# The expert stage of a four-layer network as one unrolled stream, with the gathers in fp32r

## The reference

```python
x = x + _L0_ffn_ref(_L0_cond_ref(x, cond, ...), gate_w, w1, w2)   # layer 0
x = x + _L1_ffn_ref(_L1_cond_ref(x, cond, ...), ...)             # layers 1 to 3
...
def _L0_ffn_ref(x, gate_w, w1, w2):
    probs = softmax(einsum('BTC,CE->BTE', x, gate_w))
    top_p, top_idx = top_k(transpose(probs, (0, 2, 1)), cap)   # cap = 2*32/8 = 8 tokens for each expert
    xin = take_along_axis(x[:, None], top_idx[..., None], axis=2)
    h = gelu(einsum('BElC,ECH->BElH', xin, w1))                # 8 experts, H = 512
    y = einsum('BElH,EHC->BElC', h, w2) * top_p[..., None]
    return zeros.at[b_idx, top_idx].add(y)
```

## Time and profile before

| | |
|---|---|
| time, 3 runs | median 617.47 us (617.43 to 617.65) |
| the profiled execution | 614.02 us |
| its span, first to last instruction | 612.7 us |
| mean granted TensorE clock | 0.989 of full |
| TensorE busy | 568.9 us (93%) |
| VectorE busy | 444.6 us (73%) |
| ScalarE busy | 359.5 us (59%) |
| GpSimd busy | 206.6 us (34%) |

### The profile page before, as it was taken

One profiled execution on the slowest core, in us unless ns is written; L12 is line 12 of the kernel. 1 busy time (PEld: TensorE's weight loads), 2 busy tenths in 40 slices (PEclk: granted clock), 3 DMA queues, 4 the chain that ended last, 5 costly groups with the idle time before them and its releaser, 6 DMA issues.

```text
span 612.7 us, 10503 instructions
## 1 busy us (share of the span) xinstructions
PE 568.9 (93%) x3463; PEld 486.2 (79%) x3479; DVE 444.6 (73%) x1080; ACT 359.5 (59%) x773; POOL 206.6 (34%) x200
## 2 busy tenths in 40 slices
PE   8988999999998698999899978999999999999995
PEld 7766788787876587998789967789889898988773
DVE  5966555555565767675765625998999999999965
ACT  5456666775775332443233324587677777778873
POOL 5757777877865002976100000011000000001110
PEclk9999999999998799999899999999999999999999
DMA  8613304441300341013000000000000000000001
GB/s 293 207 71 142 139 17 192 172 172 67 140 1 19 119 147 51 1 53 104 0 0 0 1 1 1 2 1 2 2 1 10 19 10 10 11 10 10 19 18 34
DMA packets 13929, 34.72 MB, mean 57 GB/s; under 512 B 3148, under 2 KB 6584, under 8 KB 12984
## 3 DMA queue, kind: packets, MB, share of 16 engines
q1 hardware_dynamic: 13880, 34.10, 15.5%
HBM read 30.24 MB, written 2.28 MB: 53 GB/s over the span
## 4 chain that ended last, share of the span: by engine, by line
PE 74%; DVE 8%; POOL 6%; ACT 5%; issue 4%; DMA 2%; SPq 1%; DVEq 0%; ACTq 0%
PE bank L366 8%; PE bank L368 7%; PE bank L367 7%; PE bank L1259 7%; PE bank L1476 4%; PE bank L1468 4%; PE bank L1555 4%; PE bank L1500 4%; PE bank L1501 3%; POOL hidden_low L418 3%; PE bank L1347 3%; PE bank L1167 2%; POOL hidden_low L982 2%; PE bank L1534 1%; PE bank L1521 1%
## 5 line engine op out<-in xcount | busy, mean ns | idle before, releaser
L418 POOL TENSOR_TENSOR hidden_low<-hidden,hidden_high 128x512 fp32r<-128x512 f32 x72 | 92.3, 1294 | 31.2 <-ACT hidden_high L413 30.4
L1832 POOL CAST h_high<-h 128x256 fp32r<-128x256 f32 x16 | 7.3, 459 | 207.5 <-ACT h L1644 207.5
L483 ACT ACTIVATE bank<-bank 128x512 f32<-128x512 f32 x56 | 32.6, 583 | 36.6 <-PE bank L368 36.4
L487 DVE TENSOR_TENSOR hidden<-bank,big 128x512 f32<-128x512 f32 x56 | 38.5, 688 | 21.4 <-ACT bank L483 20.7
L366 PE MATMUL bank<-xin_high,w_high 128*128 128x256 f32 x128 | 46.5, 363 | 6.5 <-DVE xin_low L1236 6.5
L413 ACT CAST hidden_high<-hidden 128x512 fp32r<-128x512 f32 x73 | 44.9, 615 | 3.8 <-DVE hidden L479 3.0
L1500 PE MATMUL bank<-taps_high,q1T 128*128 128x512 f32 x94 | 45.6, 486 | 0.8 <-DVE tap L1740 0.5
L1287 ACT ACTIVATE pb<-bank 128x512 f32<-128x512 f32 x32 | 19.1, 597 | 35.1 <-PE bank L368 34.9
L1501 PE MATMUL bank<-taps_low,q1T 128*128 128x512 f32 x94 | 37.0, 394 | 0.0
L1468 PE MATMUL bank<-x,lstm_wx 128*128 128x128 f32 x256 | 33.7, 275 | 2.9 <-ACT ident_bf L1449 1.9
L368 PE MATMUL bank<-xin_high,w_low 128*128 128x256 f32 x128 | 36.3, 284 | 0.0
(11 more groups left out here) (274 smaller groups left out, 1788.0 us busy)
## 6 DMA issues: line engine op xcount, KB each, us to landing
big<-gates_scratch SPq DMA_DIRECT2D x7, 2048.0 KB, 7.5
w<-in_f_w SPq DMA_DIRECT2D x16, 256.0 KB, 7.7
onehot<-topi_scratch SPq DMA_DIRECT2D x6, 512.0 KB, 3.8
outT<-x SPq DMA_DIRECT2D x16, 128.0 KB, 1.8
xT<-in_xT SPq DMA_DIRECT2D x3, 512.0 KB, 8.0
cgt<-ctok SPq DMA_DIRECT2D x6, 256.0 KB, 4.6
big<-topi_scratch SPq DMA_DIRECT2D x2, 512.0 KB, 4.4
hidden<-in_ffn_w SPq DMA_DIRECT2D x3, 256.0 KB, 2.9
```

Of the source, the lines that this page charges most:

```text
L418: pool.tensor_tensor(hidden_hl[u % 3][1][:, :], hidden[u % 3][:, :], hidden_hl[u % 3][0][:, :].bitcast(F32), ALU.subtract).then_inc(s_lo, 1)
L487: dve.tensor_tensor(hidden[u % 3][:, :].rearrange("p (i k) -> p i k", k=P), r_bank[j % 2][:, :].rearrange("p (i k) -> p i k", k=P), gate_r ...
```

## The change

It does the following.

1. Lin, `val`, the loop and the DMA copies `cgt` go; all four groups are written out as one stream of 64 units, w = 16 g + u. `expert_up` runs LEAD = 3 units ahead, across the borders of groups.
2. The tail of group g: half of the transposes (experts 0 to 3) behind unit 14, the other half behind unit 0 of group g+1, the scatter behind its unit 2. Each half is one round through both banks.
3. The choice of half 0 moves from chunk 7 to chunk 5; its loads are issued in chunk 6. The first gather moves into chunk 7, behind units 7, 9 and 10, the fourth part behind the last unit. The choice of half 1 moves into group 0.
4. A gather multiplies the high and the low part of the tokens with the one-hot rows in fp32r, into two banks; a ScalarE copy of each bank gives the high and the low part of the gathered tokens. So `expert_split` splits only weights, and the tokens are split once per half group: high part on ScalarE (in chunk 7 on VectorE), low part on VectorE. `GATHER_AFTER` is 5, 7, 9, 11.

The core of the diff (renamings, and `val(...)` around constants, left out):

```diff
@@ chunk @@
+            CHOICE_CHUNK, LAST_GATHER = 5, (7, 9, 10)
+                    if last and u in LAST_GATHER:
+                        if u == LAST_GATHER[0]:
+                            pe.wait_ge(s_q, NCHUNK * NSH - 1)
+                        gather_product(LAST_GATHER.index(u))
-                    if last and u == 3:
+                    if c == CHOICE_CHUNK and u == 3:
                         choice_exp(0)
+                    if last and u >= 10:
+                        gather_copy(u - 10)
                 if last:
                     hidden_high(c, n - 1, units[n - 1])
+                    gather_copy(2)
...
+                    if last and u in (1, 2):
+                        gather_onehot(0, u - 1)
+                    if last and u in (4, 5):
+                        tokens_high(dve, 0, u - 4)
+                        tokens_low(0, u - 4)
+                    if last and u >= 10:
+                        expert_split(u - 10)
-                    if last and u >= 9:
+                    if c == CHOICE_CHUNK and u >= 9:
                         choice_tables(0, ...)
...
+                if c == CHOICE_CHUNK:
+                    choice_store(0)
+                if c == CHOICE_CHUNK + 1:
+                    sp.wait_ge(s_vc, 32)
+                    for k in range(2):
+                        gather_loads(0, k)
+                    load_slots(0)
@@ gather, units @@
+            LEAD = 3
+            def gather_product(q):
+                g, par, b = q // 4, (q // 2) % 2, q % 2
+                pe.wait_ge(s_oh, q // 2 + 1)
+                pe.wait_ge(s_cs, 2 * (q // 2) + 2)
+                if q:
+                    pe.wait_ge(s_gx, q)
+                for i in range(2):
+                    tile = 2 * b + i
+                    slots = slice(tile * SLOT_TILE, (tile + 1) * SLOT_TILE)
+                    for half, dst in zip(tokens(g, par), gather_banks(q)):
+                        mm = pe.matmul(dst[:, i * SLOT_TILE:(i + 1) * SLOT_TILE], half[:, tile * C:(tile + 1) * C],
+                                       chosen(g, par)[:, slots], start=True, stop=True)
+                mm.then_inc(s_ga2, 1)
+            def gather_copy(q):
+                act.wait_ge(s_ga2, q + 1)
+                for k in range(2):
+                    ...
+                    cp = act.copy(..., gather_banks(q)[k][:, :].rearrange("p (i e s) -> p e i s", i=2, e=E))
+                cp.then_inc(s_gx, 1)
+            def expert_split(k):
+                e = k % E
+                if k >= 2:
+                    dve.wait_ge(s_h, 2 * k - 2)
+                high, low = w1_hl[e % 2]
+                dve.tensor_copy(high[:, :], w1[:, e, :]).then_inc(s_es, 1)
+                dve.wait_ge(s_es, 2 * k + 1)
+                dve.tensor_tensor(low[:, :], w1[:, e, :], high[:, :].bitcast(F32), ALU.subtract).then_inc(s_es, 1)
@@ stream @@
+            def group_pe(g):
+                for u in range(U2):
+                    w = g * U2 + u
+                    if w + LEAD < GROUPS * U2:
+                        expert_up(w + LEAD)
+                    if g == 0 and u == 2:
+                        pe.wait_ge(s_sce, NCHUNK)
+                    if g == 0 and u == 4:
+                        pe.wait_ge(s_ye, 1)
+                        choice_transpose(1, y_bank[0][:, SLOT_GE:SLOT_GE + P])
+                    if g == 0 and u == 8:
+                        pe.wait_ge(s_dc, TABLES + TURNED)
+                    expert_down(w)
+                    if g and u == 0:
+                        slots_turn(g - 1, 1)
+                    if g and u == 2:
+                        scatter(g - 1, 0)
+                        scatter(g - 1, 1)
+                    if g < GROUPS - 1 and u in GATHER_AFTER:
+                        ...
+                        gather_product(q)
+                    if g == 0 and u == 12:
+                        pe.wait_ge(s_gx, 8)
+                        weight_total(m_bank[1][:, 0:4])
+                    ...
+                    if u == 14:
+                        slots_turn(g, 0)
+            def group_act(g):
+                for u in range(U2):
+                    w = g * U2 + u
+                    ...
+                    act.activation(hb[w % 4][:, :], h_bank[w % 4][:, :], ACT.Gelu).then_inc(s_hg, 1)
+                    if g == 0 and u == 1:
+                        choice_exp(1)
+                    if g < GROUPS - 1 and u in (2, 6):
+                        tokens_high(act, g + 1, u // 4)
+                    if g and u == 3:
+                        slots_out(g - 1, 1)
+                    if g < GROUPS - 1 and u - LEAD in GATHER_AFTER:
+                        gather_copy(4 * (g + 1) + GATHER_AFTER[u - LEAD])
+                slots_out(g, 0)
+            def group_dve(g):
+                for e in range(E):
+                    k = g * E + e
+                    if k + 2 < GROUPS * E:
+                        expert_split(k + 2)
+                    if g and e == 1:
+                        residual(g - 1, 0)
+                        residual(g - 1, 1)
+                    if g < GROUPS - 1:
+                        if e in (1, 3):
+                            tokens_low(g + 1, e // 2)
+                        if e in (2, 4):
+                            gather_onehot(g + 1, e // 2 - 1)
+                    if e >= 4:
+                        scatter_tables(g, range(4 * (e - 4), 4 * (e - 3)))
+                    output_copy(g, e)
+                    if g == 0 and e == 0:
+                        choice_probs(1)
+                        slots_copy(0, m_bank[0])
+                    if g == 0 and e == 2:
+                        choice_tables(1, y_bank[0][:, SLOT_GE:SLOT_GE + P], (0, 1))
+                    if g == 0 and e == 3:
+                        choice_tables(1, None, (2, 3))
+                    if g == 0 and e == 5:
+                        weight_sums()
+                    if g == 0 and e == 6:
+                        weight_means(m_bank[1][:, 0:4])
-            with nc.Fori(0, GROUPS - 2) as i:
-                group(Lin(i, 1, 1))
```

More of the change, by code:

```diff
@@ new lines, in gather_onehot, with half_tokens, tokens_high @@
+            def gather_onehot(g, par):
+                dve.wait_ge(s_ld[par], 16 * (g + 1))
+                dst = chosen(g, par)
+                dve.tensor_scalar(dst, dst.bitcast(F32), part[:, 0:1], None, ALU.is_equal).then_inc(s_oh, 1)
+            def half_tokens(g, par):
+                k = 2 * g + par
+                return ctok[:, k * HALF_TILES:(k + 1) * HALF_TILES, :].rearrange("p i c -> p (i c)")
+            def tokens_high(eng, g, par):
+                k = 2 * g + par
+                if g >= 2:
+                    eng.wait_ge(s_ga2, 2 * k - 2)
+                eng.wait_ge(s_cs, 2 * k)
+                cast = eng.copy if eng is act else eng.tensor_copy
+                cast(tokens(g, par)[0], half_tokens(g, par)).then_inc(s_cs, 1)
@@ new lines, in expert_down @@
+            def expert_down(w):
+                e, b = (w % U2) // 2, w % 2
+                pe.wait_ge(s_hg, w + 1)
+                if b == 0 and w >= 4:
+                    pe.wait_ge(s_ye, w // 2 - 1)
+                for i in range(2):
+                    ht = 2 * b + i
+                    mm = pe.matmul(y_bank[e % 2][:, 0:SLOT_GE], w2[:, e, ht, :], hb[w % 4][:, i * SLOT_GE:(i + 1) * SLOT_GE],
+                                   start=(ht == 0), stop=(ht == HT - 1))
+                mm.then_inc(s_y2, 1)
@@ new lines, in slots_out, with scatter @@
+            def slots_out(g, h):
+                for b in range(2):
+                    act.wait_ge(s_yt, 4 * g + 2 * h + b + 1)
+                    if g and h == 0 and b == 0:
+                        act.wait_ge(s_so, 2 * g)
+                    dst = ysl[:, 8 * b:8 * b + 8, :].rearrange("p (i h) k -> p i h k", h=2)[:, :, h, :]
+                    act.copy(dst, m_bank[b][:, :].rearrange("p (i k) -> p i k", k=P)).then_inc(s_yl, 1)
+            def scatter(g, b):
+                pe.wait_ge(s_yl, 4 * g + 4)
+                pe.wait_ge(s_st, 2 * g + b + 1)
+                for i in range(4):
+                    tile = 4 * b + i
+                    for h in range(2):
+                        mm = pe.matmul(m_bank[b][:, i * P:(i + 1) * P], ysl[:, 2 * tile + h, :], scat[:, 2 * tile + h, :],
+                                       start=(h == 0), stop=(h == 1))
+                mm.then_inc(s_so, 1)
@@ new lines, in build_program @@
+            for w in range(LEAD):
+                expert_up(w)
+            for g in range(GROUPS):
+                group_sp(g)
+                group_pe(g)
+                group_act(g)
+                group_dve(g)
+                if g == 0:
+                    prepare_weights()
+                if g == GROUPS - 2:
+                    for k in range(3):
+                        load_tap(k)
+            slots_turn(GROUPS - 1, 1)
+            slots_out(GROUPS - 1, 1)
+            for b in range(2):
+                scatter(GROUPS - 1, b)
```

(1 more changed line is left out.)

468 lines of the change are left out of this document (189 added, 279 removed).

## The result

The changed kernel takes 598.89 us (median of 4 runs, 597.71 to 599.28), the kernel before 617.45 in the same comparison: ratio 0.9697, 95% interval 0.9681 to 0.9714. The forecast was 600.3. The profiled execution took 598.74 with a span of 597.4 (before 614.02 and 612.7).

A forecast was written before the change was run, and what follows sets the result against it. TensorE, busy 93% of the span, was taken as the bound. Savings 10.8 - 1.1 - 1.0 - 1.3 + 9.8 = 17.2 us gave 596.8 profiled; carrying 3.45 to the median gave 600.3, range 594 to 608.

The forecast's parts named there:

- Between the stages: Gap from the last chunk product to the first expert product: 14.2 us falls to 3.4, 10.8 saved.
- low clock: First expert products may still run at half rate for 1 to 5 us: 1.0 us lost, bounds 0 and 2.5.
- The exponential ... moved, so nothing: Half 0's exponential, moved from chunk 7 to 5: two table loads and TensorE's 1.33 us wait only move, net cost nothing.
- token splits: Two splits at 1.15 us, with two one-hot tables at 0.66, in chunk 7: 1.3 us lost together, bounds 0 and 2.8.
- Top-k: Half 0's top-k tables stand between units in chunk 5: 1.0 us lost, bounds 0 and 2.4.
- gather copies: Two ScalarE copies of 1.08 us each ahead of the last chunk's last two hidden casts: 1.1 us lost.
- Lead of 3 and group 0: Late weight splits cost TensorE 1.7 us in groups 1 to 3; group 0 waits 5.2, ending at 36.2.
- fp32r gathers: Each gather block in the expert groups costs TensorE 0.48 us, not 0.87: 4.7 us saved over 12 blocks.
- A: Rival: VectorE bounds the expert stream, its split 0.35 us late for all 32 experts: 607.8 us; chance 0.18.
- B: Rival: moved VectorE work hides in idle time and group 0's waits are half the predicted: 595.4 us; chance 0.20.
- C: Rival: group 0's waits make the clock fall and stay low for the group: 631 us; chance 0.04.
- D: Rival: SP's queue brings one-hot rows 8 us late in chunk 7 and again in group 0: 616.3 us; chance 0.04.

The follow-up runs named there:

- tokens_early: Changed kernel with the token splits for the first gather placed one by one in chunk 4, not in chunk 7: 596.95 us.
- x_later: Changed kernel with, in chunk 5 alone, the split of x for the next chunk behind unit 6, not unit 3: 597.25 us.
- early split: Changed kernel with VectorE splitting the weights of expert k+3, not k+2, ahead of the output copy of expert k: 592.85 us.
- lead of 2: Changed kernel with LEAD = 2 in place of 3, nothing else: 592.20 us.
- tails_end: Changed kernel with transposes, scatter and addition to x of groups 0 to 2 at the end of their own group: 608.78 us.
- best 1: Changed kernel plus early split, x_later, first three gather copies behind the last hidden cast, and half 0's top-k spread over four units: 589.75 us.
- best 2: best 1 plus tokens_early and the weight total of group 0 behind unit 13, not 12: 586.47 us.

## Why the prediction was right, and where it was not

- **Between the stages:** right, and more: 12.2 saved, not 10.8. The transposes and scores ran at clock 1.00, not 0.50; probably because the first gathers fill idle pieces ahead of the end, which no run shows by itself. The "low clock" term (1.0) did not come here either. Low clock came in chunks 5 and 6 instead (0.8), where the prediction had none.
- **"The exponential ... moved, so nothing"** is the step that failed. It cost 3.37 in chunk 5 (the run without its tables takes all of it out) and gave back 1.3 in chunk 7 (22.09 before, 20.77 in tokens_early; the 21.16 of the table holds 0.39 of the token splits): net 2.0. The nearest row had its wait in the last chunk, which has no split of a next x; in chunk 5 ScalarE's and GpSimd's parts of that split stand in the same unit. Of the 3.37 that is 1.7 (23.76 against 22.08 in x_later), low clock behind the wait 0.65 (24.41 against 23.76), and 1.0 is what the exponential costs without the split of x.
- **Top-k** measured 1.36 against 1.0, of which 0.16 is low clock (22.43 against 22.27 in early split), **gather copies** 1.0 against 1.1, **token splits** 1.85 against 1.3 together with the one-hots, whose own share was not taken apart: all near their terms, 0.8 over in all.
- **Lead of 3 and group 0:** right in mechanism and size. Predicted 4.1 for the split in group 0, 1.7 in the others and 1.0 beside GpSimd; early_split takes 6.15 out. The weight total's 1.1 measured 0.93. Group 0 ended at 36.2 from its first product, to the tenth; groups 1 and 2 took 33.6 and 33.8, not 33.0 and 32.7, and the last with its tail 37.0, not 36.9. So the 1.0 for GpSimd showed in groups 1 and 2, as 1.7. What the prediction did not say is what follows from its own sum: that a lead of 2 is better here.
- **fp32r gathers** 0.48 for a block, as said; their 4.7 is partly cover (3.4 measured). **Tails:** tails_end shows what they are worth inside the next group, 9.5.
- **Stream** 140.6 against 140.8, but the 140.8 held 1.0 of low clock that did not come; the 0.7 more of GpSimd's share fills most of that.
- **Rivals.** A is out by early_split; B is out since the token splits did not hide and group 0 took the predicted 36.2. C: the clock stayed 1.00 through group 0 in the profiled execution; it fell there in two others, at a price of 1.5 us, not for the group. D did not come, but the first half of its condition nearly did: the one-hot rows for the first gather took 10.9 us to land (the row below), 7 more than the earlier trace rows; those for the later groups took 3.6. They were issued at 158 and first used at 178.4, so TensorE never waited for them. It was the distance of a chunk that held against D, not the time to land.

```profile
onehot<-topi_scratch SPq DMA_DIRECT2D x2, 512.0 KB, 10.9
```

- **The sum.** By the marks 0.3 - 6.4 + 12.2 + 9.9 = 16.1, against 17.2: the chunks cost 3.0 more than the 3.4 predicted, and the gap between the stages gives 1.4 back. The prediction had 596.8 for the profiled execution, and 598.74 came: 1.1 of it the stage, 0.8 behind it, in the untouched layers, whose last 22 us ran at clock 0.88 (1.00 before). The carried 3.45 between profile and median did not hold for the changed kernel (0.15). So the forecast of 600.3 was only 1.4 off because two errors of 1.9 and 3.3 have opposite signs. That closeness is luck; the 16.1 against 17.2 is the measure of the reasoning.

That carry is very likely the clock. In the experiments' comparisons the kernel before took 611.18 at a mean clock of 0.994 and 618.38 at 0.981; the changed kernel's four runs have 0.992 to 0.997. For the executions of 617.4 to 617.65 no clock is on record. By this some 2.5 of the 18.6 us between the medians are clock (18.6 less the 16.1 of the trace), in fewer low stretches of the changed kernel; that it has them less often because its idle pieces of TensorE are shorter is likely and not shown.

## What to carry to other kernels

For an engine that works in program order write down when an instruction's input is ready, when its result is due, and what stands ahead of it. A longer lead of the engine that needs the result brings the due time forward, as here, and a wait for a free buffer placed too early stops all behind it. A stall that is moved keeps neither its size nor its cover: look what else ScalarE and GpSimd do in the new place. And compare clocks before carrying a distance between profile and median.

## What the hardware showed unexpectedly

- The same stall is followed by a low clock in one execution and not in another. Eight traces have the same 1.84 us wait in chunk 5; in six the clock stayed at 1.00. The changed kernel, early split and lead of 2, windows behind it:

```profile
141.10:144.70 3.60, 3.27 (x12) 2.06 (x10) 1.81 (x3) 1.19 (x2) 3.60 (x4) 0.53 0.00 0
```

```profile
141.10:144.70 3.60, 2.73 (x12) 1.94 (x13) 2.59 (x5) 1.76 (x4) 3.60 (x3) 1.00 0.00 0
```

```profile
141.00:150.00 9.00, 8.23 (x27) 6.19 (x26) 4.40 (x7) 3.33 (x6) 5.52 (x5) 0.62 0.00 0
```

0.53 is mostly the lower of the two levels (1.2 against 2.4 GHz). From the transposes inside chunk 4 to those inside chunk 6 the three take 46.84, 46.03 and 48.66, so by chance 0.8, nothing or 2.6 us more. A single profile can't price an edit below that, unless it is compared with traces of the same clock.

- Beside GpSimd an operation of VectorE that reads two SBUF tensors is not slower in proportion; it waits. GpSimd's rows above hold two differences each. In best 1 the second began at 156.16, the 32-element sum of VectorE at 156.17, and both ended within 0.1 us (157.45 and 157.50). In best 2 the sum began at 156.22, just ahead of the second difference (156.24), and took 0.19. The gated product, which reads PSUM, took 0.67 to 0.69 throughout. The Trainium skill (SBUF — State Buffer, Who interferes with whom) says that a VectorE instruction with two SBUF inputs contends with a GpSimd instruction that reads SBUF, and that this contention is an exclusive lock. The traces agree: the sum waited for the whole of GpSimd's instruction or not at all. So such an operation costs its own time or up to 1.1 us more here (1.33 against 0.19), and its start to less than a tenth of a us decides which.
